# Two kinds of ScalarE copies moved one slot later in a fused state-space scan kernel

## The reference

```
a = layernorm(x);  n = rmsnorm(a) * norm_w
skip = n @ W_skip;  xin = silu(causal_conv4(n @ W_in) + conv_b)      # 1024 channels
delta = softplus(xin @ W_delta_1 @ W_delta_2 + b);  B, C = xin @ W_B, xin @ W_C   # 16 states
h = h * exp(delta * A) + (delta * xin) * B        # step by step along the sequence
y = sum over states of h * C  + xin * W_D
x = x + layernorm(a + (y * silu(skip)) @ W_out)
g = layernorm(x);  x = x + layernorm(g * sum(top8 softmax weights) + weights @ expert_bias)
```

## Time and profile before

| | us |
|---|---|
| median of 3 runs (lowest, highest) | 2429.27 (2428.14, 2432.55) |
| profiled execution, its own time | 2422.3 |
| its span, first to last instruction | 2420.4 |
| PE busy / POOL busy | 1993.2 (82%) / 1915.9 (79%) |
| DVE busy / ACT busy | 1772.3 (73%) / 1665.3 (69%) |

### The profile page before, as it was taken

How to read it: one execution, slowest core, us unless ns; L and a number is a source line. 1 busy time by engine, 2 the same in 40 slices (tenths; PEclk the granted TensorE clock), 3 DMA queues, 4 the chain that set the end, 5 groups by cost and what they waited for, 6 DMA issues and landing times. The chain is left out here.

```text
span 2420.4 us, 35546 instructions
## 1 busy us (share of the span) xinstructions
PE 1993.2 (82%) x11717; PEld 1589.4 (66%) x11717; DVE 1772.3 (73%) x3105; ACT 1665.3 (69%) x3276; POOL 1915.9 (79%) x1192
## 2 busy tenths in 40 slices
PE   4577778898788888888888898888898888888784
PEld 3366667677576767767676776768677675767552
DVE  3377877788696867879687886968688796888632
ACT  2368786776777776687777768777766876877521
POOL 1279897897978888798888979788897988999812
PEclk9879999999999998999999999999999999999996
DMA  4555557565564646656475656647466554646320
GB/s 156 167 165 184 194 175 230 180 218 174 192 205 161 224 140 220 200 176 208 143 233 177 214 179 196 209 149 231 149 230 196 171 183 155 207 158 196 114 98 18
DMA packets 239281, 434.31 MB, mean 179 GB/s; under 512 B 19134, under 2 KB 135418, under 8 KB 239098
## 3 DMA queue, kind: packets, MB, share of 16 engines
q1 hardware_dynamic: 239098, 432.04, 55.3%
HBM read 347.57 MB, written 84.41 MB: 178 GB/s over the span
## 5 line engine op out<-in xcount | busy, mean ns | idle before, releaser
L606 POOL TENSOR_TENSOR hc<-h,c_all 128x1024 f32<-128x1024 f32 x512 | 1206.0, 2365 | 264.0 <-DVE h L945 261.7
L945 DVE TENSOR_TENSOR_SCAN h<-operand,carry,bank 128x512 f32<-128x512 f32 x480 | 592.1, 1269 | 209.1 <-ACT operand L699 111.6
L1129 PE MATMUL bank<-ident,u_t 128*128 128x128 f32 x2560 | 428.1, 293 | 276.8 <-DVE h L945 266.3
L1134 PE MATMUL y_sum<-ident,hc 128*128 128x128 f32 x4096 | 628.9, 286 | 8.8 <-POOL hc L606 6.9
L1129 PEld LDWEIGHTS bank<-ident,u_t 128*128 128x128 f32 x2560 | 304.6, 148 | 441.5 <-issue 255.0
L718 ACT ACTIVATE u_t<-dx_t,b_t 128x256 f32<-128x256 f32 x1280 | 574.5, 499 | 0.0
L1134 PEld LDWEIGHTS y_sum<-ident,hc 128*128 128x128 f32 x4096 | 512.5, 149 | 61.9 <-issue 39.2
L590 POOL TENSOR_TENSOR operand<-dx_q,b_all 128x1024 f32<-128x1024 f32 x192 | 453.7, 2363 | 16.5 <-DMA dx_q<-dx_dram 16.5
L699 ACT ACTIVATE operand<-delta_q,neg_a 128x512 f32<-128x512 f32 x640 | 430.8, 711 | 0.3
L945 DVE TENSOR_TENSOR_SCAN h<-bank,carry,operand 128x512 f32<-128x512 f32 x288 | 357.6, 1272 | 93.4 <-ACT bank L699 67.0
L699 ACT ACTIVATE bank<-delta_q,neg_a 128x512 f32<-128x512 f32 x384 | 262.2, 683 | 156.5 <-DVE h L945 154.8
(11 more groups left out here) (120 smaller groups left out, 2042.6 us busy)
## 6 DMA issues: line engine op xcount, KB each, us to landing
c_all<-bc_dram SPq DMA_DIRECT2D x256, 512.0 KB, 4.1
b_all<-bc_dram SPq DMA_DIRECT2D x192, 256.0 KB, 5.4
win<-in_L_attn_W_in SPq DMA_DIRECT2D x64, 512.0 KB, 4.6
wskip<-in_L_attn_W_skip SPq DMA_DIRECT2D x64, 512.0 KB, 4.4
x_dram<-x SPq DMA_DIRECT2D x64, 256.0 KB, 4.8
delta_dram<-delta SPq DMA_DIRECT2D x32, 512.0 KB, 5.3
dx_dram<-dx SPq DMA_DIRECT2D x32, 512.0 KB, 6.1
delta_q<-delta_dram SPq DMA_DIRECT2D x32, 512.0 KB, 5.4
```

The costliest lines, as they stand in the source:

```text
L606: nc.gpsimd.tensor_tensor(hc[:, number % 3], h[:, number % 3], c_all[:, j % 2, s % 2:s % 2 + 1].to_broadcast([P, 2, SPAN]), ALU.mult).then ...
L945: nc.vector.tensor_tensor_scan(h[:, number % 3, q], first, second, start, ALU.mult, ALU.add).then_inc(scan_done.sem, 1)
L1129: last = transpose(bank[:, q, b * P:(b + 1) * P], u_t[:, j % 2, b, q * P:(q + 1) * P], ident[:])
L1134: return matmul(to, lhsT=of, rhs=ident[:], is_transpose=True, start=start, stop=stop, skip_group_check=True)
```

## The change

ACT's `take_y` moves from the end of its slot 1 to the end of its slot 2, and from 17 to 18. `take_dxt` of the second quarter moves from the end of slots 4 and 7 to the end of slots 5 and 8. SP's `store_y` moves from slots 2 and 18 to 3 and 19. PE's, DVE's and POOL's orders are the same in both. The number of instructions that compute is the same.

```diff
@@ block.sync @@
-                        if s == 18:
+                        if s == 19:
                             store_y(t, 0)
-                        if s == 2:
+                        if s == 3:
                             store_y(t - 1, 1)
@@ block.scalar @@
-                        if s == 1:
+                        if s == 2:
                             take_y(t - 1, 1)
-                        if s == 17:
+                        if s == 18:
                             take_y(t, 0)
...
-                        if s in (4, 7):
-                            take_dxt(t, 1, s // 3 - 1)
+                        if s in (5, 8):
+                            take_dxt(t, 1, s // 8)
```

## The result

The changed kernel takes 2442.5 us (median of 8 runs, 2435.55 to 2447.09), the kernel before 2430.1 us (8 runs, 2421.18 to 2434.53): ratio 1.0049, 95% interval 1.003 to 1.0068. It is slower, by 12.4 us; 2442 was predicted.

A forecast was written before the change was run, and what follows sets the result against it. An engine-changing chain was taken as the limit, with PE bounding slots 1 to 4. Terms +4.2 (slots 2 to 6), +3.0 (slot 18), +4.5 (chunks 0, 1), +1.2 (chunks 14, 15) made +12.9: median 2442 us, range 2431 to 2453.

The forecast's parts named there:

- PE bounds slots 2 to 4, and the copy is tied to scan 2's start: Slot 2, middle chunks: L1152 cannot start sooner than 4.16 us after scan 2, so PE waits 1.42 us more.
- The dx part gives back 1.07: Scan 4 to scan 6, middle chunks: the later dx copy saves 1.07 us per chunk.
- Slot 18: 0.25: Slot 18, middle chunks: PE waits 0.25 us more for the sum's copy, +3.0 us over 12 chunks.
- The store: zero: SP's queue: the store of y behind one more load of C costs nothing.
- The sum: Whole kernel: the terms together cost +12.9 us, giving 2442 us for the median.
- Chunks 0 and 1: Three places without gate work nearby: PE waits 1.5 us more in each, +4.5 us, nothing gives it back.
- The smallest term: Chunks 14 and 15, four places: +0.3 us each, +1.2 us together, bounds 0 and 8.8.
- Rival 1, absorbed: Slots 3 to 8 may give back all of 1.42 us, and later waits absorb more: about 2433 us, chance 0.13.
- Rival 2, faster: ACT's waits were the bound and PE has slack; dx pays, y costs nothing: 2416 us, chance 0.08.
- Rival 3, the clock: More is lost: dx gives nothing back, or PE's clock falls behind new gaps, up to 26 us more; 2460, chance 0.13.

The follow-up runs named there:

- mid_only: Against the kernel before, only the sum's copy moved, to between the two halves of the decay in slots 2 and 18: 2429.7 us, ratio 0.9995.
- dx5_only: Against the kernel before, only the first of the two dx copies moved, slot 4 to 5: 2405.3 us, ratio 0.9904.
- dx_only: Against the kernel before, only the second quarter's dx copies moved, slots 4 and 7 to 5 and 8: 2405.1 us, ratio 0.9892.
- store_only: Against the kernel before, only the stores of y moved one slot later in SP's queue: 2429.6 us, ratio 0.9997.
- y_only: Against the kernel before, only the sum's copy and its store one slot later, dx copies unmoved: 2473.0 us, ratio 1.0175.
- y_fill7: Sum's copy and store later, plus slot 7's four dx turnings done three times over: 2457.2 us, ratio 1.0099 to the kernel before.
- before_fill13: The kernel before with the first output product of slot 13 done four times over: 2431.0 us, ratio 0.9993.

## Why the prediction was right

- *PE bounds slots 2 to 4, and the copy is tied to scan 2's start.* Right: 4.07 us from scan 2 to L1152 instead of 4.16, scan 2 to 4 longer by 1.40 us on average over the 12 middle chunks, 1.35 to 1.41 in each (reckoned 1.42). Scan 3's gain was lost one slot later, and mid_only, which has that gain without PE's wait, shows that it is worth nothing. The terms I had added up were 0.1 too long, so that L1152 itself is 1.33 us later; the first L1152 also took 1.13 behind its wait instead of 1.05, which makes it 1.41.
- *The dx part gives back 1.07.* Right in kind, a little small: 1.21 from scan 4 to 6 (1.17 in ten chunks, 1.41 in chunks 8 and 9), since DVE's rows follow each other more closely than I had taken, and 0.09 in slots 6 to 9. Only the first copy pays (dx5_only). PE waits nowhere for the copy in the middle chunks, as reckoned. In chunks 14 and 15 it waits 4.4 us for it, and dx_only's chunks 14 and 15 (218.0 against 218.2 us) win nothing.
- *Slot 18: 0.25.* 0.23 measured.
- *The store: zero.* Right (store_only).
- *The sum* came out right by terms that missed in both directions. For the middle chunks 12 x (1.40 - 1.30 + 0.23) = 4.0 us of waits stand against 7.2 forecast. The two traces differ there by 9.1. The remainder is mostly in the rest, where PE was at the lower clock for 11.1 us per chunk instead of 8.5 (8.2 to 10.0 in the other kernels). The lower clock is in part the change's doing: over its eight runs the mean granted clock is 0.931 in the median, and 0.936 to 0.937 in the kernel before's groups. How much of the 12.4 us it made is not shown. Chunks 0 and 1 are 7.6 us longer (4.5 forecast), but two kernels in which PE never waits for the copy there, store_only and mid_only, are 2.7 and 3.1 us longer as well, so the change's share is 4.5 to 7.6.
- *The smallest term was the worst.* Chunks 14 and 15 cost 6.2 us where I took 1.2 (the bound was 8.8), and 7.2 in y_only. The +0.3 a place was a guess without a row behind it. PE's waits there are 2.90, 2.04, 2.90 and 2.39 us, and the dx part, which I counted as help, gives nothing back.
- *Rival 1, absorbed,* falls as a mechanism: in y_only nothing of the 1.40 comes back in slots 4 to 9 (10.32 and 14.16, as before). Its number for these slots came nearer than mine, though. The dx part gives 1.30 per chunk, so that of slots 2 to 9 only 1.2 us in all are left and not 4.2. *Rival 2, faster,* falls for the change as a whole, but its dx half is real and larger than I wrote, 25 us. *Rival 3, the clock,* falls in the middle chunks: behind the new gap of 1.1 to 1.2 us L1152 took 1.13 us and ran at the full clock in all 12, and the changed kernel has no more falls at slots 8 and 14 than the kernel before. Behind the longer new gaps of chunks 14 and 15 it came true in two places of four. In chunk 14, slot 2:

```profile
2095.15 2.04 PE L1152 MATMUL y_sum<-diag_d,x_q 128*128 128x128 f32 x8 [2.90 <-ACT y_out L740]
```

The other gap of 2.90 us, in chunk 15, brought no fall (1.13). The rival's own price was too low. The clock fell at 1562.01, so the 0.87 us of the earlier trace rows lie only in part behind the fall. The next matmuls of L1129 there took 1.06 us, and the bound of 26 us should have been about 44:

```profile
1563.29 1.06 PE L1129 MATMUL bank<-ident,u_t 128*128 128x128 f32 x4
```

- *What was not foreseen.* The parts do not add up as waits. The later sum copy alone costs 43 us where 29 were reckoned from its waits, the dx part alone gives 25 where its waits give 15. The difference in the first is the clock's fall at slot 8: 9 more falls, 12.1 us between slots 9 and 10, and y_fill7 takes all of them away. In the second it goes with the falls at slot 14 (10 of 12 to 2); before_fill13 removed these falls as well, and its slots 15 to 17 are shorter, but its time does not stand out, so this half is shown by the rows only. In the changed kernel both effects are absent. For the first the rows show how: its dx part shortens the gap at slot 8 to 1.67 us, behind which no kernel had a fall. That the falls at slot 14 stayed at 10 has no explanation here. I had foreseen neither, and the parts of 43 and -25 us leave 18, not the 12.4 measured. So the mechanism at slots 2 to 6 and 18 is shown, but that the total came within 1 us of 2442 is in good part luck.

## What to carry to other kernels

The largest wait in the list of waits may be worth nothing: ACT waited 211.5 us for PE's sum, and taking that wait away changed no time that could be told. Ask what stands behind the moved instruction on the engine that waits for it, and tie its new place to the event that it will really follow; here one place further, behind a decay that waits for a scan's second half, was the difference between no cost and 1.4 us per chunk. Where two edits travel in one change, time them apart: this one held a gain of 25 us under a loss of 43. Expect that the two do not add up, since either may change the gaps in which PE's clock falls.

## What the runs showed of the hardware

The granted clock of PE depends on the gap before a stretch, and on more. Behind the gap of 1.4 to 1.7 us at slot 8 it fell in none of 66 places. Behind the same 2.57 us gap, with the same instructions around it, it fell in 10 chunks of y_only and in 1 of the kernel before, so that an edit at slot 2 moved falls at slot 8. At slot 14 a gap of 2.24 us brought a fall in 10 of 12 chunks of the kernel before and in 2 of 12 of dx_only. The Trainium skill ("TensorE: Matmul & The Clock Gate", section "HAM oscillation — how this bites in real kernels") names gaps in PE's work as the cause of the lower clock; y_fill7, where 8 needless matmuls shortened the gap to 1.70 us and the falls at slot 8 went from 10 to none, agrees. What decides between two equal gaps, of which one brings a fall and one does not, was not settled here.
